# Cross attention in fp32 on one core: four batches in flight per slot instead of three, new stage order and banks, ctx transposed by VectorE

## What is computed

```python
Mn = _conv1x1(Wn, bn, _inorm(x_c)); Mm = _conv1x1(Wm, bm, _inorm(x_s))
A = softmax(einsum('bct,bcs->bts', Mn, Mm)); Ml = _conv1x1(Wl, bl, x_s)
x1 = _conv1x1(Wo, bo, einsum('bcs,bts->bct', Ml, A)) + x_c
q = layer_norm(x1) @ q_w + q_b; k = ctx @ k_w + k_b; v = ctx @ v_w + v_b
hidden = softmax(q k^T * scale, masked) v @ cproj_w + cproj_b + x1
out = hidden + gelu(layer_norm(hidden) @ fc_w + fc_b) @ proj_w + proj_b
```

## Time and profile before

| | us |
|---|---|
| median of 3 runs (3250.63 to 3253.25) | 3251.77 |
| the profiled execution, its own time | 3251.27 |
| its span in the trace | 3249.5 |
| mean granted TensorE clock | 0.993 |
| PE / DVE / ACT / POOL busy in the span | 3183.0 / 2022.0 / 1330.3 / 714.6 |

### The profile page before, as it was taken

The page is one execution under the profiler, slowest core; times in us unless marked ns, Lnnn a source line. Parts: engine busy times, 40 slices in busy tenths (PEclk is TensorE's granted clock), DMA queues, the critical chain, the costliest instruction groups (busy, mean ns, idle before and its releaser), DMA issues. The chain is left out here.

```text
span 3249.5 us, 54148 instructions
## 1 busy us (share of the span) xinstructions
PE 3183.0 (98%) x18807; PEld 2544.8 (78%) x18807; DVE 2022.0 (62%) x4029; ACT 1330.3 (41%) x3890; POOL 714.6 (22%) x674
## 2 busy tenths in 40 slices
PE   7999999999999999999999799999999999999999
PEld 5777777777777777777777688888888888888887
DVE  6888888888888888888887543333333333333332
ACT  4565555566666666665556421111111111111111
POOL 3333333333333333333332300000000000000000
PEclk8999999999999999999999899999999999999999
DMA  2000000000000000000000321111111111111110
GB/s 85 27 29 29 29 29 29 29 29 29 29 26 29 29 29 23 29 29 29 29 29 23 114 65 39 30 22 39 39 33 32 39 39 39 39 39 39 39 26 13
DMA packets 185732, 113.81 MB, mean 35 GB/s; under 512 B 137696, under 2 KB 138208, under 8 KB 185696
## 3 DMA queue, kind: packets, MB, share of 16 engines
q1 hardware_dynamic: 185696, 113.34, 12.1%
HBM read 64.02 MB, written 33.55 MB: 30 GB/s over the span
## 5 line engine op out<-in xcount | busy, mean ns | idle before, releaser
L1185 ACT ACTIVATE gl<-pre,fc_bias 128x512 f32<-128x512 f32 x256 | 176.5, 690 | 1128.3 <-PE pre L1270 1128.3
L1224 DVE CAST hT_hi<-gl 128x512 fp32r<-128x512 f32 x256 | 109.1, 426 | 847.5 <-ACT gl L1185 847.5
L562 ACT ACTIVATE rows<-bank,negmax 128x128 f32<-128x128 f32 x1024 | 365.5, 414 | 168.0 <-DVE negmax L734 168.0
L498 POOL TENSOR_TENSOR rows<-rows,rsum 128x512 f32<-128x512 f32 x256 | 266.4, 1040 | 537.6 <-DVE rsum L740 537.6
L859 PE MATMUL bank<-ident,rows 128*128 128x128 f32 x2048 | 295.2, 277 | 29.6 <-POOL rows L498 18.9
L545 ACT ACTIVATE rows<-bank,negmax 128x512 f32<-128x512 f32 x256 | 175.0, 686 | 363.6 <-DVE negmax L704 363.6
L859 PEld LDWEIGHTS bank<-ident,rows 128*128 128x128 f32 x2048 | 235.2, 141 | 112.1 <-DVE rows L750 34.1
L1269 PE MATMUL pre<-yT_hi,rest_lo 128*128 128x512 f32 x768 | 299.2, 390 | 0.0
L1268 PE MATMUL pre<-yT_lo,rest_hi 128*128 128x512 f32 x768 | 299.0, 389 | 0.0
L1270 PE MATMUL acc<-rest_hi,hT_hi 128*128 128x512 f32 x768 | 298.9, 389 | 0.0
L1270 PE MATMUL pre<-yT_hi,rest_hi 128*128 128x512 f32 x768 | 298.8, 389 | 0.0
(11 more groups left out here) (162 smaller groups left out, 7342.5 us busy)
## 6 DMA issues: line engine op xcount, KB each, us to landing
x_in<-in_x SPq DMA_DIRECT2D x64, 256.0 KB, 2.7
ctx_in<-in_ctx SPq DMA_DIRECT2D x64, 256.0 KB, 2.9
hidden<-hid SPq DMA_DIRECT2D x64, 256.0 KB, 2.0
rows<-hidden SPq DMA_DIRECT2D x16, 1024.0 KB, 5.5
out<-rows SPq DMA_DIRECT2D x64, 256.0 KB, 2.1
stage<-y SPq DMA_DIRECT2D x240, 64.0 KB, 2.3
stage<-in_L_xattn_fc_w SPq DMA_DIRECT2D x4, 1024.0 KB, 6.5
stage<-in_L_xattn_proj_w SPq DMA_DIRECT2D x4, 1024.0 KB, 7.1
```

What stands on the lines that cost most here:

```text
L498: pool.tensor_tensor(probs[:, r, :, :], probs[:, r, :, :], rsum1[:, r, :].unsqueeze(2).to_broadcast([P, 4, P]), ALU.mult).then_inc(probs_s ...
L562: act.activation(probs[:, r, c, :], by_chunk(S1_BANK[r])[:, c, :], ACT.Exp, bias=negmax1[:, r, c:c + 1], accum_out=sum1[:, r, c:c + 1]).th ...
L1185: act.activation(gl[:, i % 2, :], pre[i % 2][:], ACT.Gelu_apprx_tanh, bias=mlp.fc_bias[:, i:i + 1]).then_inc(gelu_done, 1)
```

## The change

The pipeline over batches becomes deeper: b0 is batch s, b1 to b4 are s-1 to s-4, and slots run from -1 to 67, seven written out ahead of the loop. In one slot now run: M, S0, softmax and scaling of A for b0; A's transposes, U, out0, x1, K, V and k's transposes for b1; x1n's transposes, Q, q's transposes and S1 for b2; P, PV and C for b3; `hid` for b4. No product is split any more and all banks are new. ctx is no longer transposed by TensorE: sixteen copies of 32-column blocks per batch from HBM (`load_blocks`) put it into `blocks` block-wise, one VectorE `transpose` turns the 32x32 blocks into `ctx_t`, ScalarE takes the upper half from there and GpSimd the lower one. x for the residual is loaded a second time (`x_res`), `k_sb` is copied by ScalarE instead of VectorE, and `q_sb` shares the tile of `x1n`. The splitting of the K, V, Q and C weights moves one or two slots later.

```diff
+        x_res = small[:].rearrange("p a b -> p (a b)")
+        ctx_t = small_t[:].rearrange("p a b -> p (a b)")
+        blocks = sb("blocks", [P, T])
...
+        q_sb = x1n
...
-        S0_BANK = (5, 6, 0, 1)
-        S1_BANK = (2, 4, 5, 6)
-        AT_BANK = (1, 3, 2, 4)
-        PT_BANK = (1, 3, 5, 6)
-        FIRST, LOOPED, LAST = -1, 3, B + 1
...
+        M_BANK = (5, 6)
+        AT_BANK = (4, 0, 1, 7)
+        XN_BANK = 2
+        S0_BANK = (5, 6, 4, 0)
+        U_BANK = OUT0_BANK = 1
+        Q_BANK = QT_BANK = KT_BANK = 7
+        PT_BANK = (3, 2, 5, 6)
+        K_BANK = C_BANK = 4
+        PV_BANK = 5
+        S1_BANK = (0, 1, 2, 3)
+        V_BANK = 6
+        FIRST, LOOPED, LAST = -1, 6, B + 3
...
             def load(e):
                 if e.has_before(2):
-                    after(x1_set, (e + -2).nth(1, 1))
-                    after(ctxT_turned, (e + -2).nth(1, 1))
                     after(normed_set, (e + -2).nth(2, 2))
                 u = e.parity
...
+            def load_blocks(e):
+                if e.has_before(1):
+                    after(ctxT_turned, (e + -1).nth(1, 1))
+                to = blocks[:].rearrange("p (j c b) -> p j c b", j=DC, b=32)
+                of = ctx[e.number].rearrange("(c p) (j d b) -> p j c d b", p=32, d=4, b=32)
+                for d in range(4):
+                    for c in range(4):
+                        sp.dma_start(to[32 * d:32 * (d + 1), :, c, :], of[:, :, c, d, :]).then_inc(blocks_in, 16)
...
             load(Item(0, 0, B))
+            load_blocks(Item(0, 0, B))
...
             stage_weight(3)
+            load_blocks(Item(0, 1, B))
...
-                e = s + 1
+                e = s + -4
+                if e.exists():
+                    after(hid_set, e.nth(1, 1))
+                    sp.dma_start(hidden[e.number], hid[:, e.parity, :]).then_inc(hid_stored[e.parity], 16)
+                e = s + 2
                 if e.exists() and e.has_before(2):
                     load(e)
                 e = s + -1
                 if e.exists():
+                    if e.has_before(1):
+                        after(x1_set, (e + -1).nth(1, 1))
+                    else:
+                        sp.wait_ge(wow_copied, 2)
+                    sp.dma_start(x_res, x[e.number]).then_inc(x_res_loaded, 16)
...
-                e = s + -2
-                if e.exists():
-                    after(hid_set, e.nth(1, 1))
-                    sp.dma_start(hidden[e.number], hid[:, e.parity, :]).then_inc(hid_stored[e.parity], 16)
+                e = s + 1
+                if e.exists() and e.has_before(2):
+                    load_blocks(e)
...
+                if b0.exists():
+                    pool.wait_ge(ctxT_hi_set, b0.nth(1, 1))
+                    pool.tensor_tensor(flat(ctxT_lo), ctx_t, flat(ctxT_hi).bitcast(F32), ALU.subtract)\
+                        .then_inc(ctxT_lo_set, 1)
...
+                if b1.exists():
+                    act.wait_ge(k_done, b1.nth(1, 1))
+                    act.activation(k_sb[:], bank[K_BANK][:], ACT.Copy).then_inc(k_copied, 1)
...
+                if b0.exists():
+                    if b1.exists():
+                        act.wait_ge(v_done, b1.nth(1, 1))
+                    act.wait_ge(ctxT_turned, b0.nth(1, 1))
+                    act.activation(flat(ctxT_hi), ctx_t, ACT.Copy).then_inc(ctxT_hi_set, 1)
...
-                if e2.exists():
-                    dve.wait_ge(cproj_done, e2.nth(1, 1))
-                    dve.wait_ge(x1b_set, e2.nth(1, 1))
...
+                if b2.exists():
+                    dve.wait_ge(mask_loaded[b2.parity], b2.dma())
...
+                    dve.wait_ge(x_res_loaded, b1.nth(16, 16))
+                    dve.scalar_tensor_tensor(out=x1[:], in0=bank[OUT0_BANK][:], scalar=out0_bias[:, 0:1],
+                                             in1=x_res, op0=ALU.add, op1=ALU.add).then_inc(x1_set, 1)
...
+                if b0.exists():
+                    dve.wait_ge(blocks_in, b0.nth(256, 256))
+                    if b1.exists():
+                        dve.wait_ge(ctxT_lo_set, b1.nth(1, 1))
+                    dve.transpose(ctx_t, blocks[:]).then_inc(ctxT_turned, 1)
+                if b3.exists():
+                    dve.wait_ge(outT_hi_set, b3.nth(1, 1))
+                    lower(flat(outT_lo), bank[PV_BANK][:], flat(outT_hi), outT_lo_set)
...
-                for t in range(DC):
-                    scale_A(t)
-                max1(0)
-                if e0.exists():
-                    dve.wait_ge(k_done, e0.nth(1, 1))
-                    dve.tensor_copy(k_sb[:], bank[7][:]).then_inc(k_copied, 1)
...
-            slots(dve, slot, {0: lambda: (prepare_small(), lower_halves(K_W), prepare_vecs()),
-                              1: prepare_q, LAST: first_group})
+            slots(dve, slot, {0: lambda: (prepare_small(), prepare_vecs()), 1: lambda: lower_halves(K_W),
+                              2: prepare_q, LAST: first_group})
...
-                    if e1.exists():
-                        pe.wait_ge(kT_set, e1.nth(1, 1))
-                    pe.wait_ge(ctx_loaded[e0.parity], e0.dma())
-                    turn(bank[0], lambda c: ctx_in[:, e0.parity, c * P:(c + 1) * P], ctxT_turned)
-                    for i, b in enumerate((1, 3)):
-                        pe.wait_ge(normed_lo_set, e0.nth(2, i + 1))
+                b0, b1, b2, b3, b4 = s, s + -1, s + -2, s + -3, s + -4
+                if b0.exists():
+                    if b4.exists():
+                        pe.wait_ge(outT_lo_set, b4.nth(1, 1))
+                    if b2.exists():
+                        pe.wait_ge(v_set, b2.nth(1, 1))
+                    for i, b in enumerate(M_BANK):
+                        pe.wait_ge(normed_lo_set, b0.nth(2, i + 1))
...
+                if b1.exists():
+                    pe.wait_ge(a_scaled, b1.nth(4, 4))
+                    if b4.exists():
+                        pe.wait_ge(hid_set, b4.nth(1, 1))
+                    for j in range(DC):
+                        if j in (1, 2) and b3.exists():
+                            pe.wait_ge(exp1_done, b3.nth(16, 4 * j))
+                        if j == 3 and b2.exists():
+                            pe.wait_ge(kT_set, b2.nth(1, 1))
+                        turn(bank[AT_BANK[j]], lambda t: A[:, t, j * P:(j + 1) * P], at_turned)
+                if b2.exists():
+                    pe.wait_ge(x1n_set, b2.nth(1, 1))
+                    if b3.exists():
...
+                if b1.exists():
+                    pe.wait_ge(ctxT_lo_set, b1.nth(1, 1))
+                    pe.wait_ge(at_lo_set, b1.nth(4, 3))
+                    for j in range(DC):
+                        if j == 3:
+                            pe.wait_ge(at_lo_set, b1.nth(4, 4))
...
+                if b1.exists():
+                    pe.wait_ge(u_lo_set, b1.nth(1, 1))
+                    three_passes(bank[OUT0_BANK][:], small_hi[:, 2, :], small_lo[:, 2, :], u_hi[:], u_lo[:])\
+                        .then_inc(out0_done, 1)
+                if b3.exists():
+                    pe.wait_ge(exp1_done, b3.nth(16, 16))
+                    for r in range(4):
+                        pe.wait_ge(probs_set, b3.nth(4, r + 1))
+                        if r >= 2 and b0.exists():
+                            pe.wait_ge(exp0_done, b0.nth(4, r - 1))
+                        turn(bank[PT_BANK[r]], lambda c: probs[:, r, c, :], pT_turned)
+                if b2.exists():
...
+                if b1.exists():
+                    if not b1.has_before(1):
+                        pe.wait_ge(w_lo_set[K_W], 4)
+                    if b0.exists():
+                        pe.wait_ge(exp0_done, b0.nth(4, 3))
+                    project(bank[K_BANK], ctxT_hi, ctxT_lo, K_W, k_done)
...
+                if b2.exists():
+                    pe.wait_ge(mask_set, b2.nth(1, 1))
+                    pe.wait_ge(qT_set, b2.nth(1, 1))
+                    if b0.exists():
+                        pe.wait_ge(exp0_done, b0.nth(4, 4))
+                    if b1.exists():
+                        pe.wait_ge(x1_set, b1.nth(1, 1))
+                    else:
+                        pe.wait_ge(kT_set, b2.nth(1, 1))
...
+                    project(bank[V_BANK], ctxT_hi, ctxT_lo, V_W, v_done)
+                    pe.wait_ge(k_copied, b1.nth(1, 1))
+                    if b2.exists():
+                        pe.wait_ge(qT_set, b2.nth(1, 1))
+                    turn(bank[KT_BANK], lambda c: k_sb[:, c * P:(c + 1) * P], kT_turned)
...
+            slots(pe, slot, {0: prepare_small, 2: prepare_q_bias})
```

More of the change, by code:

```diff
@@ L448, in load_for_mlp @@
                     sp.dma_start(stage[:, n, :, :], mlp_stage_source(w, n)).then_inc(mlp.staged[n], 16)
-            slots(sp, slot, {B: load_for_mlp})
+            slots(sp, slot, {B + 1: load_for_mlp})
         @block.gpsimd
@@ L685, in slot @@
                     dve.bn_stats(in_stats[:, 1, :], ctx_in[:, u, :]).then_inc(in_stat, 1)
+                if b1.exists():
```

(32 more changed lines are left out.)

429 lines of the change are left out of this document (149 added, 280 removed).

## The result

| | before | after |
|---|---|---|
| median of the runs, us | 3251.2 (3249.0 to 3253.25) | 3181.21 (3180.42 to 3181.92) |
| ratio to before | | 0.9784, 95% interval 0.9771 to 0.9797 |
| span of the profiled execution, us | 3249.5 | 3179.3 |
| one slot, from `x1b` to `x1b`, us | 27.71 | 26.005 |
| start of the MLP part, us | 1831.56 | 1760.28 |

70 us faster, and 9 us slower than the forecast of 3172. The middle gave more than forecast (64 x 1.705 = 109.1 us for 96.6), the two ends took more back (37.8 us for 17). The MLP part is as long as before (1419.0 for 1417.9).

The account below looks back on a forecast made before the run. TensorE bounds the kernel: 25.9 us of work plus 0.3 of waits make a 26.2 us slot instead of 27.71. 64 slots save 96.6, less 17 at start and end: 3172 us, range 3155 to 3195 (chance 0.53).

Parts of the forecast that it names:

- The leftover waits: TensorE in a slot: 0.3 us of waits stay on top of 25.9 us of work, giving 26.2.
- the collisions: VectorE's A scaling, normalisation and x1n are delayed beside GpSimd operations: 0.9 us together per slot, making the loop 25.5.
- the loop's sum: Loop through VectorE (15.5 us) and ScalarE with the rest (9.1): 24.6 us a slot without collisions.
- handovers: TensorE's waits for other engines' results: 1.4 us of the old 27.71 us slot, mostly gone after the change.
- Rival A: The VectorE/ScalarE loop binds with full collisions: slot 26.7 to 27.6 us, 3230 us at 27.1; chance 0.25.
- Rival B: Long transpose runs lower TensorE's clock: slower, slot 28.2 us, 3300 us; chance 0.07.
- Rival C: No waits left over: slots of 25.8 to 25.9 us, a start costing 10, 3147 us; chance 0.10.
- Rival D: Block copies land late and VectorE's transpose waits every slot: 3288 us at 28 us for sixteen copies; chance 0.05.
- Transfers: SyncE's sixteen block copies per slot take 7.5 us, bounds 7 to 11.2, covered in the slot at either bound.
- Start and end: The two ends of the attention part cost 17 us more, bounds 5 and 30: +7, +6, +1 and +3.
- thin slots: At the start, the first slots are longer chains with less work in them: +1 us.
- what would show it: Trace signs: slot 26.2 us, gapless transposes, VectorE about 86% busy, MLP near 1752; wrong if ends took over 90 us.

Follow-up runs that it names:

- pe_plus1: Changed kernel with one more 512-column matmul per batch on TensorE, ahead of K's twelve: 3198.1 us, slot 26.273 us.
- ctx_pe: Changed kernel with ctx transposed by TensorE again, behind V, without block copies; the order of four batches in a slot stays: 3190.29 us, slot 26.473 us.
- dve_plus1: Changed kernel with one more 512-column maximum per slot on VectorE, ahead of outT_lo: 3181.09 us.
- dve_plus3: Changed kernel with three more 512-column maxima per slot on VectorE, ahead of outT_lo: 3230.03 us, slot 26.80 us.
- split_xn: Changed kernel with x1n's four transposes moved out of a run of twenty, behind S0's matmuls: 3186.71 us, slot 26.084 us.
- blocks4: Changed kernel with each batch's blocks loaded by four copies of 64 KB instead of sixteen of 16 KB: 3175.19 us.
- small_first: Changed kernel with batch 0's block copies issued behind the small weights, vectors and batch 1's loads instead of ahead: 3170.42 us.
- x_first: Changed kernel with batch 2's x and ctx issued ahead of the third and fourth weights and batch 1's block copies: 3175.79 us.
- stats_early: Changed kernel with the MLP's first statistics on VectorE ahead of outT_lo in the last slot but one: 3174.8 us.
- all repairs: Changed kernel with loads reordered, fourth weight's rounding later and MLP statistics early: 3157.98 us with four block copies a batch, 3156.76 with sixteen.

## Why the prediction was right, and where it was off

**What bounds the kernel: right.** A TensorE operation costs its whole price in every slot (`pe_plus1`, `ctx_pe`), a VectorE operation nothing up to 0.94 us (`dve_plus1`, `dve_plus3`).

**The slot: 26.2 forecast, 26.005 measured.** Two terms were off and one missed.
- TensorE's work was put at 25.9. It is 26.0. From 1022.91 to 1048.92 the 81 matmuls take 19.23 us; 0.47 of it are five starts that come 0.09 to 0.10 later than the rest, and without them one takes 0.232 (0.2314 in the earlier trace rows). The forecast had four of these, 0.36. The fifth stands between K's last matmul and PV, 0.33 instead of 0.23 us:

```profile
1040.30 0.40 PE L827 MATMUL bank<-first_hi,ctxT_hi 128*128 128x512 f32 x1
1040.63 1.08 PE L943 MATMUL bank<-y,v_sb 128*32 128x128 f32 x32
```

- The leftover waits, 0.3, do not exist. They were a margin for a loop thought to be 0.4 under TensorE's work. The step that failed is the collisions, put at 0.9: A's scaling and the normalisation met none (0.48 and 0.55 us a piece), only `x1n` kept 0.37 (0.91 against 0.54). 24.6 + 0.4 = 25.0, and `dve_plus3` measures 25.06. So the loop's sum was good and its collision term twice too large; that the two agree to 0.06 is partly luck, since the loop that `dve_plus3` stretched closes mostly through `hid` and A's transposes, not through `m_lo` and S0 as in the sum.
- Where the 1.705 us came from was told wrongly. "0.4 less work" and 1.1 of handovers was the forecast's split. `ctx_pe` gives 0.468 for ctx's four transposes, and by `split_xn`'s 0.079 the six fewer runs beyond that are worth up to about 0.5 (an estimate, six times 0.079); at the forecast's own prices they were worth nothing, since a run of four with its return (0.35 + 0.09) cost as much as four more in a run (4 x 0.11). That leaves some 0.8 for the handovers; 0.34 of it is idle time in the window of before (18.9 us in 1560, 27.71 a slot).

**Rival A fell,** with collisions of 0.4. **Rival B fell:** clock 1.00 over 1510 us with two runs of twenty transposes in each slot. **Rival C** was right that no waits are left in the slot, 0.1 short on its length (25.8 to 25.9 for 26.0) and wrong on the start. **Rival D fell:** the transpose of blocks waits for nothing in a slot.

**Transfers: right that they are covered, the price too low.** "16 x 0.47 = 7.5, bounds 7 to 11.2": 10.33 us at the start, and in the slot

```profile
1015.97 11.82 SPq L412 DMA_DIRECT2D blocks<-in_ctx  x16
```

0.65 to 0.74 each. The row of the MLP part's copies, 0.70 each, which I had taken as a bound because they carry four times as much, was the better price. The Trainium skill's rule ("DMA: Bandwidth & Descriptors", section "Rules for kernel authors": under 64 KB mostly overhead) gave the same bound. `blocks4` shows that the rule taken to the letter goes too far here: a 64 KB copy in 128-byte pieces cost 1.05 to 2.0 us of the queue, the 16 KB one 0.65 to 0.74.

**Start and end: 17 forecast, bounds 5 to 30, 37.8 measured.** This is the step that failed. Its terms against the runs:
- Small weights behind the block copies: 7 forecast, 10.4 later in the queue, 10.8 given back by `small_first` (12.2 in the trace). The price of an issue was mis-sized, 0.47 for 0.65.
- Batch 2's x behind the second sixteen: 6 (0 to 9) forecast, a wait of 9.3 on TensorE. What stood behind the same copies, batch 0's residual x, was missed: `x_first` gave back 5.4, and the rest only with that load moved as well.
- "The MLP part starts at once behind it" was wrong by 5 us: 9.23 instead of 4.18, VectorE's order at the end, shown by `stats_early`. I had priced what TensorE does there and not followed VectorE's queue, in which the statistics and `y` stand ahead of the last `hid`.
- Slot 3's S0 waits 3.54 us for `m_lo`, since ScalarE rounds the fourth weight ahead of m_hi. With the rounding moved (and the other repairs) the wait is 1.46. Missed.
- The remaining 15 to 16 us (73.3 to 74.6 against 58.2) stay with all repairs. Forecast for it were 1 for thin slots and 3 for P and PV. With sixteen copies 12.4 us of it are idle time of TensorE in the first 180 us (37.2 against 24.8), while the end idles less than before (13.5 against 15.1 in 70.28 us). The clock does not explain it: in that profile it is 0.96 in the first 180 us, 0.94 before. The longest wait left there that the kernel before does not have stands ahead of batch 1's M, first in the change, then with the repairs:

```profile
43.81 0.80 PE L825 MATMUL bank<-normed_lo,small_hi 128*128 128x512 f32 x1 [7.08 <-POOL normed_lo L529]
...
32.94 0.79 PE L829 MATMUL bank<-normed_lo,small_hi 128*128 128x512 f32 x1 [7.08 <-POOL normed_lo L533]
```

In VectorE's new order batch 1's normalisation stands behind batch 0's four maxima and A's scaling, and TensorE's program has nothing between batch 0's S0 and this M. So the term for thin slots, +1, was mis-sized. What a repair of this wait would give, no run shows.

The signs "what would show it" named came as written for the runs of transposes, the waits of the weight loads, the transpose's 0.70 us and S0 of the first batch (31.48, forecast 29); VectorE is busy for 85% of the slot (22.17 of 26.00), forecast 86%; "start and end over 90 us" was named as an error, and is one.

## What to carry to other kernels

Where one engine is the bound, price its operations by distances between starts, then sum the longest loop through the other engines and ask how much room it leaves: here 0.94 us, which a few added operations can test. A deeper pipeline with longer runs pays in the middle and is paid for at the ends, so follow every queue there, SyncE's copies and VectorE's last operations included; putting loads in the order in which they are needed gave back 10.8 and 5.4 us, each tried alone, and the order of two operations at the end 4 to 6. A resource that is free in the loop (sixteen issues under a slot's cover) is not free where nothing covers it: moving ctx to VectorE gave 30 us and its copies took 22.

## What the runs showed of the hardware

- Sixteen copies of 16 KB in 128-byte pieces hold SyncE's queue for 10.2 to 11.8 us, four of 64 KB with the same pieces for 4.2 to 7.8: neither a price per issue nor one per byte.
- Four VectorE scalings beside four GpSimd subtractions took 1.4 us each instead of 0.48 at the end of the attention part, while A's scaling beside one `in_rstd` lost nothing (0.48) and GpSimd's `in_rstd` took 0.91 us instead of 0.71: there the GpSimd operation was the longer one, not VectorE's. Why the one case differs from the other was not tested.
- Runs of twenty 128x128 transposes, twice in 26 us among 81 matmuls of 512 columns, leave the granted clock at 1.00 over 1510 us (its higher level, 2.4 GHz).
